# Sparse attention by query tiles: one tile and eight heads a unit, in 32-row strips

## Chip, core and metric

The kernel runs on one core of a Trainium2 chip. Its time is the device time of one launch in microseconds. A core has TensorE (matrix products into PSUM), VectorE, ScalarE, GpSimd and SyncE (which issues the transfers); each takes its own queue in order and waits on semaphores. TensorE's weight loads have rows of their own (PEld).

## What is computed

A decoder of two layers over 8 sequences of 256 tokens of 128 features. The part in question is the sparse self-attention of the second layer, 16 heads of 8 features each, on the normalised X:

```python
cols = np.arange(k_len)
rows = np.arange(k_len)[:, None]
strided = cols % STRIDE >= STRIDE - C          # STRIDE 128, C 8
local = cols[None, :] // STRIDE == rows // STRIDE
causal = cols[None, :] <= rows
layout = (strided[None, :] | local) & causal
...
qkv = hidden_states @ W_attn + b_attn
scores = jnp.where(mask, jnp.einsum('bhqd,bhkd->bhqk', q, k) * scale, mask_value)
attn = jax.nn.softmax(scores, axis=-1)
out = jnp.einsum('bhqk,bhkd->bhqd', attn, v)
return out @ W_proj + b_proj
```

A query of a sequence's first 128 tokens sees the keys before it in its own tile. A query of the second 128 sees those of its tile and, besides, the last 8 keys of the first tile: the far keys. The result is added to X and normalised.

## The kernel before

Two sequences are a group; four groups run one after the other, each with 512 tokens in four tiles of 128. A group has the stages memory attention, first mixture, sparse attention, cross-attention, second mixture. Every engine's program is written out by hand, with semaphores between them; a count waited for is the number of increments so far.

Sparse attention before (from L766 for TensorE, L1236 for ScalarE, L1834 for VectorE, L1517 for GpSimd): queries, keys and values of all tokens are made by three products of 512 columns; ScalarE writes qT (L1240) and kT (L1243), feature by token. Then a loop of eight steps runs over pairs of heads hh and hh + 8 (u is 0 and 1). For a head, VectorE masks the queries to the head's eight features (L1836), TensorE puts the mask into two banks (bf16, 272 columns, L787) and adds the scores of four tiles, 136 keys each, of which 8 are far keys (L791). VectorE takes the maxima of four tiles in one operation (L1841). ScalarE makes four exponentials of 136 columns, each with its maximum as bias and its sum as a by-product (L1249, two instructions each). TensorE turns the four tiles of probabilities (L799), ScalarE copies them out of PSUM (L1085), and TensorE multiplies them by values masked to two heads (L811), which GpSimd prepares in each step (L1519). VectorE besides keeps the reciprocals of the sums (L1847, L1851) and the far columns (L1848). After the loop the far columns (L842) and the reciprocals (L846) are turned, the far product is added, the output is scaled (L1899) and projected (L496), and moments (L1585, L1588), root (GpSimd, L1441 and L1443) and normalisation (L1593) give the next X. Behind that TensorE projects keys and values for cross-attention (L750, L756).

A fp32 product is two matmul instructions, a bf16 product or an fp32 transpose one. Cross-attention works already with 64-row pieces: scores at L872, transposes at L890.

## Time and profile before

| | |
|---|---|
| median of 3 runs | 1216.9 us (1215.03 to 1217.23) |
| profiled execution | 1212.65 us, span 1210.9 us |
| mean granted TensorE clock | 0.975 |
| busy: TensorE, VectorE, ScalarE, GpSimd | 1083.6, 736.4, 707.4, 184.4 us |
| TensorE's share of the span | 89% |
| chain that ended last | TensorE 50%, issue 32%, ScalarE 6%, VectorE 5% |

The span runs from the first to the last instruction; the time of an execution is a little longer. Busy times are sums of instructions and say nothing of the order: for that, the timeline (instructions in order of time, equal ones merged) and windows (busy time in a stretch, with the granted clock of TensorE, 1.00 at full speed) are read. A matmul's duration contains its way through the array: of a run of them, only the last one's counts in full, the others follow at a shorter distance.

### The profile page before, as it was taken

What the parts mean: (1) busy time and instruction counts of PE and PEld (TensorE: products, weight loads), DVE (VectorE), ACT (ScalarE), POOL (GpSimd) and SP (SyncE); (2) the same over time, 40 slices, a digit from 0 to 9 for tenths busy, and PEclk for the clock granted to TensorE, in tenths of its full rate; (3) what the DMA queues carried; (4) which work ended last, traced back from release to release, by engine and by line L of the source; (5) the groups of instructions that cost most, each with busy time, mean ns of one, the idle gap of its engine ahead of it and who ended that gap; (6) DMA issues with size and microseconds to landing.
All of it is one profiled execution on the core that took longest, in us unless ns stands there. A gap on an engine that the chain in (4) does not pass through costs nothing.

```text
span 1210.9 us, 23834 instructions
## 1 busy us (share of the span) xinstructions
PE 1083.6 (89%) x8477; PEld 714.9 (59%) x8477; DVE 736.4 (61%) x2015; ACT 707.4 (58%) x1913; POOL 184.4 (15%) x299
## 2 busy tenths in 40 slices
PE   3789998998989998999798999899979999899957
PEld 1564684554765487455586458555567647745546
DVE  5642575888643265788754237588874417667861
ACT  3361496775654176778455238677755507777724
POOL 4320120212120022022111012020212002200000
PEclk9899999999899999999899999999989999999979
DMA  7400000000000000000000000000000000000000
GB/s 221 138 1 1 1 0 1 11 19 2 1 11 1 0 1 1 10 19 1 2 1 10 1 1 0 1 11 19 2 1 10 1 1 1 0 1 2 2 1 9
DMA packets 21061, 15.59 MB, mean 13 GB/s; under 512 B 871, under 2 KB 18644, under 8 KB 20956
## 3 DMA queue, kind: packets, MB, share of 16 engines
q1 hardware_dynamic: 20956, 14.24, 4.0%
q8 instruction: 59, 0.97, 0.3%
q14 instruction: 46, 0.38, 0.1%
HBM read 13.18 MB, written 1.05 MB: 12 GB/s over the span
## 4 chain that ended last, share of the span: by engine, by line
PE 50%; issue 32%; ACT 6%; DVE 5%; POOL 3%; POOLq 2%; DVEq 1%; SPq 1%; DMA 0%; ACTq 0%
PE ps L718 10%; PE ps L872 5%; PE ps L791 4%; PE ps L908 4%; PE ps L756 3%; PE ps L890 3%; PE ps L750 3%; PE ps L811 2%; PE ps L799 2%; PE ps L747 2%; POOL rstd L1443 2%; ACT arena L1280 2%; PE ps L917 1%; PE ps L731 1%; DVE nmax L1911 1%
## 5 line engine op out<-in xcount | busy, mean ns | idle before, releaser
L1085 ACT ACTIVATE arena<-ps 128x512 f32<-128x512 f32 (+2 forms) x336 | 170.3, 535 | 112.7 <-PE ps L890 56.4
L1911 DVE TENSOR_REDUCE nmax<-ps 128x1 f32<-128x512 f32 x256 | 163.9, 683 | 25.0 <-PE ps L872 24.5
L1280 ACT ACTIVATE arena<-ps,nmax 128x512 f32<-128x512 f32 x256 | 173.6, 685 | 7.9 <-DVE nmax L1911 4.8
L890 PEld LDWEIGHTS ps<-ident,arena 64*128 64x128 f32 x2048 | 76.5, 138 | 82.8 <-issue 42.2
L1916 DVE COPY arena<-ps 128x512 f32<-128x512 f32 x128 | 88.2, 689 | 61.0 <-PE ps L890 61.0
L718 PE MATMUL ps<-big,w1a 128*128 128x512 f32 x256 | 117.3, 603 | 0.0
L890 PE MATMUL ps<-ident,arena 64*128 64x64 f32 x2048 | 92.4, 228 | 11.9 <-ACT arena L1085 6.3
L1249 ACT ACTIVATE arena<-ps,snm 128x136 f32<-128x136 f32 x256 | 91.8, 375 | 5.6 <-DVE snm L1841 5.6
L1441 POOL TENSOR_TENSOR vare<-mv,eps_ln 128x2 f32<-128x2 f32 x64 | 13.5, 210 | 477.0 <-DVE mv L1588 476.4
L718 PEld LDWEIGHTS ps<-big,w1a 128*128 128x128 f32 x256 | 46.3, 189 | 57.5 <-issue 56.5
L1226 ACT ACTIVATE big<-ps 128x512 f32<-128x512 f32 x16 | 9.6, 597 | 116.1 <-PE ps L718 116.1
L791 PE MATMUL ps<-kT,arena 128*128 128x136 f32 x512 | 77.2, 279 | 0.0
L1808 DVE TENSOR_TENSOR big<-XT,ps 128x512 f32<-128x512 f32 x32 | 22.0, 687 | 90.4 <-PE ps L702 90.3
L1920 DVE SCALAR_TENSOR_TENSOR X<-ps,cross_inv,X 128x128 f32<-128x128 f32 x256 | 72.5, 342 | 3.3 <-issue 0.5
L791 PEld LDWEIGHTS ps<-kT,arena 128*128 128x128 f32 x512 | 68.8, 190 | 1.8
L756 PEld LDWEIGHTS ps<-xwT,ctxT 128*128 128x128 f32 x512 | 61.9, 192 | 9.6 <-issue 9.6
L750 PE MATMUL ps<-ctxT,xwT 128*128 128x512 f32 x128 | 65.5, 626 | 0.2 <-ACT ctxT L1085 0.2
L756 PE MATMUL ps<-xwT,ctxT 128*128 128x128 f32 x512 | 64.2, 276 | 0.0
L1519 POOL TENSOR_TENSOR arena<-V,pair_mask 128x512 f32<-128x512 f32 x32 | 34.4, 1076 | 132.1 <-PE ps L811 95.9
L1841 DVE TENSOR_REDUCE snm<-ps 128x4 f32<-128x544 f32 x64 | 46.4, 724 | 11.3 <-PE ps L791 8.4
L1249 ACT ACTIVATION_READ_ACCUMULATOR arena<-ps,snm 128x1 f32 x256 | 53.1, 207 | 0.0
L1443 POOL TENSOR_TENSOR rstd<-vare,neg_half 128x2 f32<-128x2 f32 x72 | 51.1, 710 | 10.2 <-issue 0.2
(354 smaller groups left out, 2113.0 us busy)
## 6 DMA issues: line engine op xcount, KB each, us to landing
ctx<-in_ctx_dram SPq DMA_DIRECT2D x4, 512.0 KB, 4.2
w1a<-in_L_ffn_W_dram SPq DMA_DIRECT2D x1, 2048.0 KB, 9.7
w1b<-in_L_ffn_W_dram SPq DMA_DIRECT2D x1, 2048.0 KB, 12.1
w2b<-in_L_ffn_W_dram SPq DMA_DIRECT2D x8, 256.0 KB, 6.8
X<-in_x_dram SPq DMA_DIRECT2D x4, 256.0 KB, 2.8
out_dram<-Y SPq DMA_DIRECT2D x4, 256.0 KB, 2.4
arena<-in_L_xattn_Wq_dram SPq DMA_DIRECT2D x1, 512.0 KB
arena<-in_L_xattn_Wk_dram SPq DMA_DIRECT2D x1, 512.0 KB
```

The source lines that it names most:

```text
L718: last = pe.matmul(bank(acc[h]), w1a[:, e, h * P:(h + 1) * P], XE[:, e % 2, :], start=(e == 0), stop=(e == E - 1))
L750: pe.matmul(bank(b), xwT[:, 1, j, :], ctxT[:, seq * CTX:(seq + 1) * CTX], start=True, stop=True)\
L756: last = pe.matmul(ps[:, b, k * P:(k + 1) * P], ctxT[:, c * P:(c + 1) * P], xwT[:, 2, j, :], start=True, stop=True)
L791: last = pe.matmul(ps[:, o, c:c + KW], qm[:, u, b * SEQ + tq * P:b * SEQ + (tq + 1) * P], kT[:, k0:k0 + KW], start=False, stop=(tq == QT - 1))
L890: last = pe.transpose(ps[:, 4 + u, o:o + DK], cprob[r, 2 * (t % 2) + h, k * P:(k + 1) * P], ident[r, r])
L1085: return act.activation(dst, src, ACT.Copy)
L1249: last = act.activation(SP_[:, u, t, :], ps[:, 2 * u + t // QT, c:c + KW], ACT.Exp, bias=snm[:, u, t:t + 1], accum_out=srs[:, u, t:t + 1])
L1280: act.activation(cprob[:, 2 * (t % 2) + h, :], bank(2 * (t % 2) + h), ACT.Exp, bias=nmax[:, s:s + 1], accum_out=rsum[:, j % 2, s:s + 1]).t ...
L1443: return pool.tensor_tensor(result[:, r], with_eps[:, r], neg_half[:, r], ALU.pow)
L1911: dve.tensor_reduce(nmax[:, s:s + 1], bank(s % 4), AX.X, ALU.max, negate=True)\
L1916: dve.tensor_copy(cprobT[:, 2 * (t % 2), :], bank(4)).then_inc(cT_even, 1)
L1920: last = dve.scalar_tensor_tensor(out=X1[:, t, :], in0=ps[:, b, t * D:(t + 1) * D], scalar=cross_inv[:, j % 2, 2 * t + h:2 * t + h + 1], i ...
```

## The change

The loop over pairs of heads goes. The unit of work becomes one tile of 128 queries and eight heads, 1024 score columns in two banks; eight units make a group, in the tile order 1, 0, 3, 2 (SP_ORDER). The 128 features are four strips of 32 rows with four heads each (QUAD). Per tile, the keys are laid out four times, each masked to one head of every strip (km, GpSimd, the first tile by VectorE). Scores of a strip are a product over 32 rows with 512 columns, on top of the causal mask put in by a bf16 product. VectorE takes the maxima of 8 x 128 columns and subtracts them for all 1024 columns into SBUF; ScalarE makes one exponential of 1024 columns without bias and sum, in place. Far scores of all heads are one product per sequence; their maxima are joined by a minimum of negated maxima. Probabilities are turned in 64-row halves, 16 transposes a unit, into two banks, and copied by one ScalarE operation of 1024 columns. Values are masked into four tensors (VQ, GpSimd). Output columns come strip by strip in products with 32 stationary columns, once with the values and once with ones (quad_ones, head_ones), so that TensorE also makes the sums. VectorE divides tile by tile; the projection runs for a sequence when its two tiles are done. The addition of the bias to X moves from VectorE to GpSimd. The masks' setup changes accordingly. The diff, cut to the new stage:

```diff
-KW = CB + P
+STRIPS, QUAD = 4, 4
+SW = P // STRIPS
+UNITS = 2 * TT
+SP_ORDER = (1, 0, 3, 2)
...
+        SP_ = [sparse_c(2 * QUAD, P) for _ in range(2)]
+        spT = [sparse_c(2 * TOK) for _ in range(3)]
+        km = [sparse_c(QUAD * P) for _ in range(2)]
+        def by_half(view):
+            return view.rearrange("p (w h q) -> p w h q", w=2, h=2 * QUAD)
+        s_nmax = sb("s_nmax", [P, TT, NH])
+        far_nmax = sb("far_nmax", [P, GROUP, NH])
...
+                def far_scores_of():
+                    pe.wait_ge(far_keys_ready, it + 1)
                     for b in range(GROUP):
...
+                        t = b * QT + 1
+                        last = pe.matmul(ps[:, 4, b * P:(b + 1) * P], qT[:, t * P:(t + 1) * P], far_keys[:, b, :],
+                                         start=True, stop=True)
+                    last.then_inc(far_ps, 1)
+                def mask_scores(u):
+                    if u >= 2:
+                        pe.wait_ge(s_arg, it * UNITS + u - 1)
+                    for s in (2 * (u % 2), 2 * (u % 2) + 1):
+                        pe.matmul(bank(s), ident_bf[:, :], causal[:, :].unsqueeze(1).to_broadcast([P, QUAD, P]),
+                                  start=True, stop=False)
+                def scores(u):
+                    n = u // 2
+                    t = SP_ORDER[n]
+                    if n == 0:
+                        pe.wait_ge(km_first, it + 1)
+                    else:
+                        pe.wait_ge(km_ready, it * (TT - 1) + n)
+                    for s in (2 * (u % 2), 2 * (u % 2) + 1):
+                        r = slice(s * SW, (s + 1) * SW)
+                        last = pe.matmul(bank(s), qT[r, t * P:(t + 1) * P],
+                                         km[n % 2][r, :], start=False, stop=True)
                     last.then_inc(s_ps, 1)
...
+                def turn_probs(u):
+                    pe.wait_ge(s_exp, it * UNITS + u + 1)
+                    if u:
+                        pe.wait_ge(sT_ready, it * UNITS + u)
+                    else:
+                        pe.wait_ge(far_ready, it + 1)
+                    for i in range(2 * QUAD):
+                        for w in range(2):
+                            r = slice(w * DK, (w + 1) * DK)
+                            last = pe.transpose(ps[:, 4 + w, i * DK:(i + 1) * DK], SP_[u % 2][r, i, :], ident[r, r])
                     last.then_inc(sT_ps, 1)
...
+                def turn_far(n):
+                    b = SP_ORDER[n] // QT
+                    pe.wait_ge(g_exp, it * GROUP + b + 1)
+                    if n == 0:
+                        pe.wait_ge(v_ready, it + 1)
+                    else:
+                        pe.wait_ge(oT_ready, it * TT + n - 1)
+                    pe.transpose(ps[:, 6, 2 * P:3 * P], G[:, b, :], ident[:, :]).then_inc(gT_ps, 1)
+                def values(n):
+                    t = SP_ORDER[n]
+                    b, far, o = t // QT, t % QT == 1, 6 + n % 2
+                    pe.wait_ge(sT_ready, it * UNITS + 2 * n + 2)
+                    if n == 0:
+                        pe.wait_ge(vq_ready, it + 1)
+                    if n >= 2:
+                        pe.wait_ge(oT_ready, it * TT + n - 1)
+                    if far:
+                        pe.wait_ge(gT_ready, it * GROUP + b + 1)
+                    for c in (0, P):
+                        for i in range(QUAD):
+                            for s in range(STRIPS):
+                                r = slice(s * SW, (s + 1) * SW)
+                                moving = by_half(spT[(2 * n + s // 2) % 3])[:, :, (s % 2) * QUAD + i, :]
+                                last = pe.matmul(ps[r, o, c:c + P], quad_ones[:, i, :] if c else VQ[i][:, t, r], moving,
+                                                 start=(i == 0), stop=(i == QUAD - 1 and not far))
+                        if far:
+                            last = pe.matmul(ps[:, o, c:c + P],
+                                             head_ones[:, :, :].rearrange("p h c -> p (h c)") if c else Vg[:, b, :],
+                                             GT[:, b, :], start=False, stop=True)
                     last.then_inc(so_ps, 1)
...
+                def project(seq):
+                    pe.wait_ge(oT_ready, it * TT + (seq + 1) * QT)
+                    if seq == 0:
+                        pe.wait_ge(s_arg, it * UNITS + UNITS - 1)
+                    token_major_seq(1 + seq, qT, wproj[:, :], seq).then_inc(proj_ps, 1)
                 pe.wait_ge(qk_ready, it * 2 + 2)
...
+                mask_scores(0)
+                far_scores_of()
+                scores(0)
+                mask_scores(1)
+                scores(1)
+                for u in range(UNITS):
+                    n = u // 2 - 1
+                    turn_probs(u)
+                    if u % 2 == 0 and n >= 0 and SP_ORDER[n] % QT == 1:
+                        turn_far(n)
+                    if u + 2 < UNITS:
+                        mask_scores(u + 2)
+                        scores(u + 2)
+                    if u % 2 == 0 and n >= 0:
+                        values(n)
+                project(0)
+                values(TT - 1)
+                project(1)
...
+                def exps(u):
+                    act.wait_ge(s_arg, it * UNITS + u + 1)
+                    act.activation(SP_[u % 2], SP_[u % 2], ACT.Exp).then_inc(s_exp, 1)
+                def turned(u):
+                    act.wait_ge(sT_ps, it * UNITS + u + 1)
+                    if u >= 3:
+                        act.wait_ge(so_ps, it * TT + (u - 3) // 2 + 1)
+                    copy(spT[u % 3], ps[:, 4:6, :].rearrange("p b n -> p (b n)")).then_inc(sT_ready, 1)
+                def far_exps(b):
+                    act.wait_ge(g_arg, it * GROUP + b + 1)
+                    act.activation(G[:, b, :], G[:, b, :], ACT.Exp).then_inc(g_exp, 1)
+                def far_turned(b):
+                    act.wait_ge(gT_ps, it * GROUP + b + 1)
+                    copy(GT[:, b, :], ps[:, 6, 2 * P:3 * P]).then_inc(gT_ready, 1)
+                act.wait_ge(far_ps, it + 1)
+                copy(far_scores, ps[:, 4, 0:GROUP * P].rearrange("p (b n) -> p b n", b=GROUP)).then_inc(far_ready, 1)
+                exps(0)
+                for u in range(UNITS):
+                    n = u // 2
+                    if u + 1 < UNITS:
+                        exps(u + 1)
+                    if u % 2 == 0 and SP_ORDER[n] % QT == 1:
+                        far_exps(SP_ORDER[n] // QT)
+                    turned(u)
+                    if u % 2 == 0 and n and SP_ORDER[n - 1] % QT == 1:
+                        far_turned(SP_ORDER[n - 1] // QT)
...
+                def keys_of_tile(n):
+                    t = SP_ORDER[n]
+                    pool.tensor_tensor(km[n % 2].rearrange("p (i k) -> p i k", i=QUAD),
+                                       kT[:, t * P:(t + 1) * P].unsqueeze(1).to_broadcast([P, QUAD, P]),
+                                       quad_mask[:, :].unsqueeze(2).to_broadcast([P, QUAD, P]), ALU.mult)\
+                        .then_inc(km_ready, 1)
+                pool.wait_ge(qk_ready, it * 2 + 2)
+                for b in range(GROUP):
+                    k0 = b * SEQ + P - CB
+                    last = pool.tensor_tensor(far_keys[:, b, :].rearrange("p (h c) -> p h c", c=CB),
+                                              kT[:, k0:k0 + CB].unsqueeze(1).to_broadcast([P, NH, CB]),
+                                              head_mask[:, :].unsqueeze(2).to_broadcast([P, NH, CB]), ALU.mult)
+                last.then_inc(far_keys_ready, 1)
+                keys_of_tile(1)
                 pool.wait_ge(v_ready, it + 1)
...
+                by_head = "p t (h d) -> p t h d"
+                for i in range(QUAD):
+                    last = pool.tensor_tensor(VQ[i].rearrange(by_head, h=NH), V[:, :, :].rearrange(by_head, h=NH),
+                                              quad_heads[:, i:i + 1, :].unsqueeze(3).to_broadcast([P, TT, NH, HD]),
+                                              ALU.mult)
+                last.then_inc(vq_ready, 1)
+                pool.wait_ge(s_ps, it * UNITS + 2)
+                keys_of_tile(2)
+                pool.tensor_tensor(NHAT[:, :, :], X[:, :, :], bproj_bc[:, :].unsqueeze(1).to_broadcast([P, TT, D]),
+                                   ALU.add).then_inc(base_ready, 1)
+                pool.wait_ge(s_ps, it * UNITS + 4)
+                keys_of_tile(3)
...
+                def unit(u):
+                    n, w = u // 2, u % 2
+                    t = SP_ORDER[n]
+                    nm = s_nmax[:, n, w * 2 * QUAD:(w + 1) * 2 * QUAD]
+                    scored = ps[:, 2 * w:2 * w + 2, :].rearrange("p b (i k) -> p (b i) k", k=P)
+                    dve.wait_ge(s_ps, it * UNITS + u + 1)
+                    dve.tensor_reduce(nm, scored, AX.X, ALU.max, negate=True)
                     dve.drain()
...
+                    if t % QT == 1:
+                        dve.tensor_tensor(nm, nm, far_nmax[:, t // QT, w * 2 * QUAD:(w + 1) * 2 * QUAD], ALU.min)
+                        dve.drain()
+                    if u >= 2:
+                        dve.wait_ge(sT_ps, it * UNITS + u - 1)
+                    dve.tensor_tensor(SP_[u % 2], scored, nm.unsqueeze(2).to_broadcast([P, 2 * QUAD, P]), ALU.add)\
+                        .then_inc(s_arg, 1)
+                def far(n):
+                    b = SP_ORDER[n] // QT
+                    by_key = "p (h c) -> p h c"
+                    dve.tensor_tensor(G[:, b, :].rearrange(by_key, c=CB), far_scores[:, b, :].rearrange(by_key, c=CB),
+                                      s_nmax[:, n, :].unsqueeze(2).to_broadcast([P, NH, CB]), ALU.add).then_inc(g_arg, 1)
+                def divided(n):
+                    t, o = SP_ORDER[n], 6 + n % 2
+                    r = slice(t * P, (t + 1) * P)
+                    dve.wait_ge(so_ps, it * TT + n + 1)
+                    dve.reciprocal(kT[:, r], ps[:, o, P:2 * P])
+                    dve.drain()
+                    dve.tensor_tensor(qT[:, r], ps[:, o, 0:P], kT[:, r], ALU.mult).then_inc(oT_ready, 1)
+                def add_attention(seq):
+                    dve.wait_ge(proj_ps, it * GROUP + seq + 1)
+                    dve.tensor_tensor(half_of(Y, seq), half_of(NHAT, seq), half_of(tiles(1 + seq), seq), ALU.add)
+                    dve.drain()
+                    moments(Y, seq).then_inc(var_ready, 1)
+                def attended(seq):
+                    dve.wait_ge(rstd_ready, it * (LNS * GROUP) + 3 * GROUP + seq + 1)
+                    normalised(Y, X, seq).then_inc(layer_done, 1)
                 dve.wait_ge(xT_ready, it * 5 + 3)
                 for b in range(GROUP):
                     last = dve.tensor_copy(XTg[:, b, :, :], XT[:, b * SEQ + P - CB:b * SEQ + P].unsqueeze(1)
                                            .to_broadcast([P, NH, CB]))
                 last.then_inc(xg_ready, 1)
...
+                dve.wait_ge(qk_ready, it * 2 + 2)
+                t = SP_ORDER[0]
+                for i in range(QUAD):
+                    last = dve.tensor_scalar(km[0][:, i * P:(i + 1) * P], kT[:, t * P:(t + 1) * P], quad_mask[:, i:i + 1],
+                                             None, ALU.mult)
+                last.then_inc(km_first, 1)
+                dve.wait_ge(qkv_ps, it * 4 + 4)
+                dve.tensor_tensor(V[:, :, :], tiles(7), bv_bc[:, :].unsqueeze(1).to_broadcast([P, TT, D]), ALU.add)
+                dve.tensor_tensor(Vgb.rearrange("p b h d -> p b (h d)"),
                                   ps[:, 6, 0:GROUP * D].rearrange("p (b d) -> p b d", b=GROUP),
...
+                                  bv_bc[:, :].unsqueeze(1).to_broadcast([P, GROUP, D]), ALU.add).then_inc(v_ready, 1)
+                dve.wait_ge(far_ready, it + 1)
+                dve.tensor_reduce(far_nmax[:, :, :], far_scores.rearrange("p b (h c) -> p b h c", c=CB), AX.X, ALU.max,
+                                  negate=True)
+                for u in range(UNITS):
+                    unit(u)
+                    if u == 0:
+                        dve.tensor_tensor(Vg.rearrange("p b (h d) -> p b h d", h=NH), Vgb,
+                                          head_mask[:, :].unsqueeze(2).unsqueeze(1).to_broadcast([P, GROUP, NH, HD]),
+                                          ALU.mult)
+                    if u % 2 and SP_ORDER[u // 2] % QT == 1:
+                        far(u // 2)
+                    if u in (4, 6):
+                        divided((u - 4) // 2)
+                divided(2)
+                dve.wait_ge(base_ready, it + 1)
+                add_attention(0)
+                divided(3)
+                attended(0)
+                add_attention(1)
+                attended(1)
```

## Rows read from the trace of the kernel before

**Rows 1.** Windows: busy us of each engine (count), granted clock, DMA; first sparse-attention stage.

```profile
144.86:191.23 46.37, 42.75 (x394) 37.00 (x394) 32.61 (x98) 35.97 (x150) 10.48 (x12) 1.00 0.00 1
```

**Rows 2.** Timeline of that stage: start, us, engine, line, operation, count, idle before.

```profile
144.17 0.69 ACT L1243 ACTIVATE kT<-ps,cols 128x512 f32<-128x512 f32 x1 [0.17 <-PE ps L774]
...
165.52 1.09 PE L811 MATMUL ps<-arena 128*64 128x128 f32 x16
...
169.89 1.09 PE L811 MATMUL ps<-arena 128*64 128x128 f32 x16
...
186.91 0.42 DVE L1903 TENSOR_TENSOR Y<-NHAT,ps 128x256 f32<-128x256 f32 x1 [0.80 <-PE ps L496]
...
187.96 0.25 DVE L1588 BATCH_NORM_AGGREGATE mv<-bn 128x2 f32<-128x6 f32 x2
...
189.37 0.60 DVE L1593 TENSOR_SCALAR X<-Y,mv,rstd 128x128 f32<-128x128 f32 x2
...
190.63 0.60 DVE L1593 TENSOR_SCALAR X<-Y,mv,rstd 128x128 f32<-128x128 f32 x2 [0.67 <-POOL rstd L1443]
```

**Rows 3.** Groups by line and form, ScalarE: count, busy us, mean ns, idle before.

```profile
L1085 ACT ACTIVATE arena<-ps 128x512 f32<-128x512 f32 x216 | 129.1, 599 | 77.3 <-PE ps L890 56.4 <-PE ps L799 12.3 <-PE ps L756 4.5
...
L1085 ACT ACTIVATE arena<-ps 128x768 f32<-128x768 f32 x8 | 6.4, 800 | 0.0
...
L1129 ACT ACTIVATE big<-big 128x512 f32<-128x512 f32 x8 | 5.0, 631 | 0.0
```

**Rows 4.** The same groups for VectorE, and two lines of its timeline.

```profile
L1691 DVE RECIPROCAL alpha<-big 128x256 f32<-128x256 f32 x8 | 13.4, 1722 | 0.1
...
L1761 DVE TENSOR_REDUCE lg_nmax<-ps 128x1 f32<-128x768 f32 x8 | 7.7, 957 | 9.3 <-PE ps L629 9.3
...
L1761 DVE TENSOR_REDUCE lg_nmax<-ps 128x1 f32<-128x640 f32 x8 | 6.6, 824 | 17.7 <-PE ps L629 17.7
...
L1883 DVE TENSOR_TENSOR V<-ps,bv_bc 128x512 f32<-128x512 f32 x4 | 2.7, 680 | 0.0
...
359.08 0.82 DVE L1761 TENSOR_REDUCE lg_nmax<-ps 128x1 f32<-128x640 f32 x1 [2.50 <-PE ps L629]
...
359.98 0.16 DVE L1763 TENSOR_TENSOR nmax<-lg_nmax,lg_scale 128x1 f32<-128x1 f32 x1
```

**Rows 5.** TensorE's timeline: mask and scores before; cross-attention's scores and turns.

```profile
169.22 0.28 PE L787 MATMUL ps<-sparse,ident_bf 128*128 128x272 bf16 x1
...
169.33 0.63 PE L791 MATMUL ps<-kT,arena 128*128 128x136 f32 x4
...
194.41 1.99 PE L872 MATMUL ps<-X,arena 64*128 64x512 f32 x8
197.10 0.46 PE L890 MATMUL ps<-ident,arena 64*128 64x64 f32 x8 [0.70 <-ACT arena L1280]
```

**Rows 6.** GpSimd by line, and TensorE's first matmul in its timeline.

```profile
L1519 POOL TENSOR_TENSOR arena<-V,pair_mask 128x512 f32<-128x512 f32 x32 | 34.4, 1076 | 132.1 <-PE ps L811 95.9 <-DVE V L1883 36.2
...
L1510 POOL TENSOR_TENSOR nTok<-NHAT,normw_bc 128x128 f32<-128x128 f32 x16 | 6.8, 454 | 5.4 <-DVE NHAT L1754 5.4
...
13.24 0.37 PE L508 MATMUL ps<-ident,col_rows 78*128 78x78 f32 x1 [13.24 <-DMA fwr<-in_L_attn_ffn_wr_dram]
```

**Rows 7.** Windows: little of TensorE, the stretch that followed (twice); an idle one without.

```profile
298.70:300.20 1.50, 0.00 (x0) 0.00 (x0) 1.35 (x7) 0.00 (x0) 0.01 (x1) 1.00 0.00 0
300.20:310.40 10.20, 6.42 (x22) 4.69 (x23) 7.06 (x36) 4.39 (x6) 3.06 (x5) 0.50 0.00 0
643.40:645.00 1.60, 0.08 (x1) 0.00 (x0) 0.05 (x1) 0.60 (x1) 0.46 (x1) 0.99 0.58 164
645.00:648.40 3.40, 2.91 (x7) 1.78 (x8) 0.90 (x5) 1.74 (x4) 1.69 (x4) 0.50 0.01 2
354.00:356.00 2.00, 0.00 (x0) 0.00 (x0) 0.38 (x2) 0.60 (x1) 0.37 (x1) 1.00 0.45 135
```

## What the change does to the time: the prediction

> **What bounds the kernel now.** I read first the four sparse-attention stages as windows [rows 1], then one of them in order of time. In the stage shown, and to within 0.7 us in the other three, TensorE is busy 42.75 of 46.4 us, at full clock; ScalarE has 36, VectorE 32.6. So four times 46.4, 185.5 us of the 1210.9, stand to be changed, and TensorE fills 92% of them. I start a stage where kT is written (144.86 in the first) and end it where the second sequence's X is normalised (191.23), both in [rows 2]: 46.37 us. What comes before and behind stays. Inside, the loop over eight pairs of heads has a period of 4.37 us (value products start at 165.52 and 169.89 [rows 2]), 35 us in all. The reader is to see how little slack any engine has there: TensorE always finds the next head's scores to do while ScalarE makes its eight short exponentials.
>
> **What is removed.** The whole loop over pairs of heads: per group 64 short exponentials with their sums, 16 maxima, the masking of queries and values, the copies of sums and far columns. ScalarE's and VectorE's work falls. That says little about the time: the new stage has to be followed along its hand-overs, because the code allows only two units in flight and each engine takes its queue in order.
>
> **What one new unit costs.** A unit is one query tile and eight heads, 1024 columns; eight units a group.
> VectorE: the maximum of 1024 columns from PSUM. 640 took 0.824 and 768 took 0.957 us, 1.04 ns a column [rows 4], so 1.22. The subtraction: an addition from PSUM of 512 columns took 0.680 [rows 4], and with the same slope it is 1.21. With the drain between them (0.08, from an end at 359.90 to a start at 359.98 [rows 4]) a unit is 2.5 us; in the tiles that also see the far keys a minimum, like the 0.16 of a small operation [rows 4], and a drain come in, 2.75.
> ScalarE: exponential without bias, 0.631 for 512 columns; the copies took 0.599 and 0.800 for 512 and 768, 0.8 ns a column [rows 3]. So exponential 1.04, copy 1.01.
> TensorE: two bf16 mask products of 512 columns. One of 272 gives way to the next product after 0.11 us (169.22 to 169.33 [rows 5]), so 0.21 each, 0.43 for both. Scores: two fp32 calls of 512 columns, in different row strips. The 64-row calls of cross-attention run in pairs, eight matmuls (four calls) in 1.99 us of which 0.62 is the last one's length: 0.43 us per pair of matmuls, 0.87 for the unit [rows 5]. Thirty-two-row strips are not in the trace; I take them as these, with the bounds nothing and twice as much. Turning: 16 transposes; eight in cross-attention end 0.46 us after their start, 0.23 of it the last one's own length, so 0.033 apart [rows 5], so 0.53. A unit is 1.83 us.
> Value products and sums: per tile 32 fp32 calls, 64 matmuls, of 32 columns by 128. The old ones of 64 columns come 16 in 1.09 us [rows 2], 0.054 apart once one's own length of some 0.28 is taken off (four full-width fp32 score matmuls of 136 columns, 0.12 apart, end 0.63 after their start [rows 5]): two run beside each other. If four run beside each other it is 0.027; yet no weight load and matmul in the trace come closer than the 0.033 of the transposes, and I take this, 2.1 us a tile, 2.54 with the far keys' two calls. Bounds: 0.027 and 0.054 apart (1.7 and 3.5 us a tile); none beside another would be 6.9. A tile's division: reciprocal 1.722 for 256 columns, of which some 0.17 doesn't grow, as in the small operation, so 0.95 for 128 [rows 4]; with drain and product 1.32.
> GpSimd: the far keys 2 x 0.45, masked keys and values about 1.08 each [rows 6]. The four masked value tensors (4.3 us) are wanted only by the first value products, 17 us in: hidden, and the next tile's keys too. Setup operations moved on GpSimd roughly cancel: memsets and selects of the old masks go, small products for the new ones come. Its first root then shifts by under 0.5 us, and TensorE does not begin before 13.2 us, when the weights land [rows 6]: nothing.
>
> **The chain of the new stage, from kT's end.** The one rule that decides: ScalarE's queue has exponential u+1 ahead of copy u, and TensorE's transposes of u+1 wait for copy u. VectorE's next maximum waits for the scores behind these transposes. So units go round all the engines.
> (a) Far keys, their scores, first scores, hand-overs: 2.6; unit 0 2.75, the far values' mask 0.42, unit 1 2.75: 8.6 us.
> (b) Exponential 1 1.04, far exponential 0.3, copy 0 1.01, transposes, mask and scores 3 1.83 and 0.3 of hand-over, unit 3 2.5: 15.7.
> (c) Exponential 3, copy 2, far copy 0.28 (values 0 wait for it), values 0 2.54, transposes 3, mask and scores 5 1.83, unit 5 2.75, hand-overs: 25.5.
> (d) As (b), with 5 to 7: 32.6.
> (e) Exponential 7, copy 6, far copy, 35.1; values 2 37.6; division 39.2; projection 0.43 and values 3 41.8; division 43.4; projection 44.1; addition and moments 1.27, root 1.16, normalising 0.6: 47.1. The last two are from the stage before (moments' end at 188.21, normalising from 189.37 for 0.60 [rows 2]); addition and moments took 1.30 there, from 186.91 to 188.21.
> Before it is 46.4. At full clock a group is 0.7 us longer; the values' rate moves it by -1.2 to +4.0, because three value products lie on the chain. For changes of array shape, which I cannot price but by nothing and some 0.1 us each, I add 0.6: +1.3, 5 us for four groups.
> The page TensorEngine Tiling (Array Packing) of the Trainium skill, section Theoretical Speedup, puts 32-column tiles at up to four times; by it the values are 0.027 apart and the four groups come 5 us lower. No 32-column tile is in the trace.
>
> **The clock.** On this chain TensorE has about 25 us of work in 47, against 42.8 busy now. It stands idle about 2.9 us before transposes 0, 2.6 before 1, 2.6 before values 0 and 3.9 before values 2. In the kernel before, 1.5 and 1.6 us in which TensorE did almost nothing were followed by a granted clock of 0.50, its lower level (1.2 of 2.4 GHz), for 10.2 and 3.4 us [rows 7]; two more falls are like the first. Once 2 us without a matmul passed at full clock [rows 7]. With four such gaps a group I expect one or two falls in each. TensorE's share of the chain in (b) to (e) is 13.5 us, and at half clock it doubles; if 30% of it lies in such stretches it is 4 us a group, 16 in all (bounds nothing and 30).
> The page TensorE: Matmul & The Clock Gate of the Trainium skill, section on HAM oscillation, says the same of bursts between waits: the array goes back to the low clock in the pauses. The trace agrees with its 10.2 us stretches. It speaks against a change that thins out TensorE's work.
>
> **Sum.** The profiled execution took 1212.65 us, 1.75 more than its span, and lies 0.35% below the median of 1216.9; the difference of 5 + 16 = 21 is worked out on it (1234) and set on the median: 1238. As the chain's first gap may be shortened by work that I take too long, I put 1236.
>
> **Rivals.**
> Forecast, chance 0.55: bound by the hand-overs, and the clock falls: 1224 to 1250.
> The clock stays up, 0.17: 1222 (1215 to 1224). For it: the 2 us that passed unpunished. Against: four longer gaps a group.
> The narrow products do not run four beside each other, 0.13: at 0.054 apart +16 more, and the longer chain at low clock: 1250 to 1262. One at a time it would be +57 (4.7 us by three by four), which the pairs of [rows 5] speak against.
> Faster, 0.15: VectorE is the bound and not the round trip. Its work is 21 us for eight units, 5.3 for four divisions, 1 for the rest; with 2.6 ahead and 10 behind the last unit (exponential, transposes, copy, values 3, division, projection, norm), less the two divisions counted twice, a group takes 37.5 us, 9 less: 1181, and 1195 to 1208 if half of the round trips stay. It decides from where scores u+2 are ready before VectorE has done unit u+1; by my terms they come 1.7 us late once and 0.4 late later, and values 0 hold a unit back by 3 us. If the change does not give the engines the order that I read (if copy u is not behind exponential u+1), this is where it goes.
>
> **How the numbers follow.** Measuring tells no less than 0.2% from no change, 2.4 us: 1214.5 to 1219.3. Faster: 0.15, and 0.02 of the second case. Same: 0.07, the lower part of the second case. Slower: 0.76. The range leaves out most of the fourth case and the top of the third: 1206 to 1258.
>
> **What would show it.** In the windows of the changed kernel: a stage of 50 to 53 us between kT and X; TensorE busy in two thirds of it or less, idle before the first transposes of units 0 and 1 and before value products 0 and 2, waiting for ScalarE; windows with a clock of 0.50 in each stage. Exponential and copy of 1024 columns at 1.04 and 1.01, maximum at 1.22, subtraction at 1.21; 64 value matmuls in about 2.1 us. I am wrong if scores u+2 always stand before unit u+1 ends, if the clock is 1.00 throughout, or if the maxima come out clearly shorter than a slope of 1.04 ns a column.

## The result and the profile after

The changed kernel takes 1254.5 us (median of 4, 1253.0 to 1255.8) against 1216.0 beside it on the same chip: 1.032 times the time before, 95% interval [1.031, 1.034]. The direction and the range of the prediction held; the size did not: 38.5 us more, where 19 were forecast.

The profiled execution took 1254.65 us, span 1252.9, 42.0 us more than the span before. (The medians differ by only 38.5, because the profiled execution of before, 1212.65 us, lies below its median and that of after on its own.) TensorE's busy time is 1091.0 us, 7 more than before, ScalarE's 645.0 (62 less), VectorE's 740.2, the mean granted clock 0.930 instead of 0.975. The work fell where it was meant to, and the time rose.

First the four stages, from kT's end to the second X, as windows (stretch, its length, busy us of TensorE, weight loads, VectorE, ScalarE and GpSimd with counts, granted clock, DMA), then the first one cut at the ends of units 1, 3, 5 and 7, the steps (a) to (e) of the prediction:

```profile
146.64:202.03 55.39, 42.16 (x474) 24.16 (x472) 34.36 (x52) 20.18 (x26) 11.14 (x14) 0.78 0.01 1
446.33:502.22 55.89, 43.26 (x474) 24.87 (x472) 34.35 (x52) 20.17 (x25) 11.15 (x14) 0.76 0.00 1
746.60:802.55 55.95, 43.31 (x474) 24.90 (x472) 34.38 (x52) 20.18 (x25) 11.15 (x14) 0.76 0.01 1
1044.17:1099.69 55.52, 42.11 (x474) 24.26 (x472) 34.27 (x52) 20.18 (x25) 11.14 (x14) 0.78 0.01 1
...
146.64:157.57 10.93, 7.56 (x44) 2.97 (x42) 10.60 (x14) 2.73 (x4) 8.33 (x9) 0.89 0.00 0
157.57:166.57 9.00, 6.83 (x45) 3.13 (x45) 5.10 (x6) 4.13 (x5) 1.04 (x1) 0.50 0.00 0
166.57:178.36 11.79, 11.22 (x136) 6.21 (x140) 6.49 (x9) 4.21 (x5) 0.00 (x0) 0.76 0.01 3
178.36:185.58 7.22, 4.68 (x91) 2.89 (x83) 6.16 (x8) 4.13 (x5) 0.00 (x0) 1.00 0.00 0
185.58:202.03 16.45, 11.87 (x170) 8.97 (x170) 6.02 (x19) 4.97 (x7) 1.78 (x4) 0.79 0.01 2
```

These answer [rows 1]: 46.4 us at clock 1.00 have become 55.4 to 56.0 at 0.76 to 0.78. The four stages hold 37.3 of the 42.0 us (222.75 less 185.44). TensorE's 42.2 busy us are hardly fewer than the 42.75 of before, but many of them are half-clock microseconds. The granted clock is 0.50, the lower of its two levels (1.2 of 2.4 GHz), in all of (b), and in parts of (a), (c) and (e).

The second view is the timeline of the same stage, first TensorE, then VectorE: the bracket is the idle time before an entry and who ended it. It answers [rows 2, 5].

```profile
154.34 0.71 PE L827 MATMUL ps<-ident,arena 64*128 64x64 f32 x16 [2.80 <-ACT arena L1278]
...
155.75 2.07 PE L814 MATMUL ps<-arena,qT 32*128 32x512 f32 x4
160.00 1.11 PE L827 MATMUL ps<-ident,arena 64*128 64x64 f32 x16 [2.17 <-ACT arena L1116]
...
168.97 0.65 PE L854 MATMUL ps<-arena,X 128*32 128x128 f32 x8 [0.57 <-ACT q_den L1116]
...
187.98 0.66 PE L854 MATMUL ps<-arena,X 128*32 128x128 f32 x8 [3.79 <-ACT q_den L1116]
```

```profile
146.67 2.08 DVE L1939 TENSOR_SCALAR arena<-kT,quad_mask 128x128 f32<-128x128 f32 x4 [3.32 <-ACT kT L1274]
...
151.29 0.61 DVE L1900 TENSOR_TENSOR s_nmax<-s_nmax,far_nmax 128x8 f32<-128x8 f32 x1
...
153.11 1.11 DVE L1953 TENSOR_TENSOR ctx<-ctx,head_mask 128x256 f32<-128x256 f32 x1
...
155.43 0.93 DVE L1900 TENSOR_TENSOR s_nmax<-s_nmax,far_nmax 128x8 f32<-128x8 f32 x1
156.43 1.23 DVE L1904 TENSOR_TENSOR arena<-ps,s_nmax 128x1024 f32<-128x1024 f32 x1
...
164.14 1.22 DVE L1897 TENSOR_REDUCE s_nmax<-ps 128x8 f32<-128x1024 f32 x1 [3.74 <-PE ps L814]
```

TensorE's gaps stand where the prediction put them, before the turns of units 0 and 1 and before the value products of steps 0 and 2, each ended by ScalarE. The scores of unit 2 (L814) already take 2.07 us; at full clock they take 1.13. The VectorE lines hold the surprise: the masked keys, the minimum and the far values' mask take two to six times as long as beside an idle GpSimd (run 3), and [rows 4] had led to 0.16 us for the minimum.

The large operations, grouped by form (count, busy us, mean ns of one, idle before), answer [rows 3, 4]:

```profile
L1904 DVE TENSOR_TENSOR arena<-ps,s_nmax 128x1024 f32<-128x1024 f32 x32 | 39.2, 1225 | 2.4
L1897 DVE TENSOR_REDUCE s_nmax<-ps 128x8 f32<-128x1024 f32 x32 | 39.1, 1222 | 29.4 <-PE ps L814 29.3
L1917 DVE RECIPROCAL kT<-ps 128x128 f32<-128x128 f32 x16 | 15.3, 955 | 43.7 <-PE ps L857 39.8 <-PE ps L854 3.9
...
L1278 ACT ACTIVATE arena<-arena 128x1024 f32<-128x1024 f32 x32 | 33.8, 1057 | 81.7 <-DVE arena L1904 81.7
L1116 ACT ACTIVATE arena<-ps 128x1024 f32<-128x1024 f32 x32 | 32.3, 1009 | 31.9 <-PE ps L827 31.9
```

The other 4.7 us lie outside: kT of the first group ends 1.8 us later, the time from the first stage's end to the next kT is 1.7 longer, the rest is 0.7 and less. The first 1.8 are in the set-up, which the change hardly touches. TensorE there got less clock in the changed kernel (0.64, second line) than in the one before (0.80, first line). Run 10 below, whose set-up is that of the changed kernel, got 0.77 (third line) and wrote kT at 145.54 us instead of 146.64, so some 1.1 of the 1.8 us came with the execution and not with the change.

```profile
36.00:48.00 12.00, 9.54 (x56) 8.09 (x57) 5.50 (x16) 4.03 (x14) 5.38 (x9) 0.80 0.69 167
```

```profile
36.00:48.00 12.00, 10.06 (x52) 8.98 (x53) 5.22 (x16) 3.43 (x12) 5.55 (x9) 0.64 0.72 174
```

```profile
36.00:48.00 12.00, 8.83 (x53) 7.80 (x54) 6.20 (x17) 3.43 (x13) 4.82 (x8) 0.77 0.69 166
```

The 1.7 us are clock as well. Here is the way from a stage's end to the next kT, the first and the second of the kernel before, then the first of the changed one:

```profile
191.24:433.85 242.61, 224.14 (x1708) 138.63 (x1708) 148.59 (x402) 139.32 (x323) 34.19 (x54) 0.98 0.02 6
480.21:724.42 244.21, 225.99 (x1708) 139.56 (x1708) 148.72 (x402) 139.42 (x323) 34.19 (x54) 0.97 0.02 6
```

```profile
202.03:446.33 244.30, 226.29 (x1713) 140.04 (x1713) 147.97 (x401) 139.50 (x324) 34.16 (x54) 0.97 0.02 6
```

At the same place of the three, some 165 us behind the stage's end, the granted clock was 1.00 (354 to 360 us), 0.72 (643 to 649) and 0.66 (366 to 371). The kernel before had this fall on the second way alone and took 1.6 us more there. The changed kernel had it on the first as well. Run 1, with the same program there, did not, and took 242.55 us.

### The profile page after: what moved, and what is told of

It reads as the page before. It is cut to its first block, busy times and chain, and to the rows that moved or that the text cites. A ratio compares the mean times of both kernels' runs of the same rounds, so it can differ in the third digit from the quotient of the medians.

```text
span 1252.9 us, 23065 instructions
## 1 busy us (share of the span) xinstructions
PE 1091.0 (87%) x8805; PEld 671.4 (54%) x8805; DVE 740.2 (59%) x1827; ACT 645.0 (51%) x1413; POOL 186.1 (15%) x313
## 4 chain that ended last, share of the span: by engine, by line
issue 58%; PE 23%; POOL 7%; DVE 4%; ACT 4%; POOLq 2%; DVEq 1%; SPq 1%; DMA 0%; ACTq 0%
PE ps L903 4%; PE ps L939 4%; PE ps L921 3%; POOL rstd L1482 3%; PE ps L726 2%; PE ps L755 2%; ACT arena L1316 2%; DVE nmax L1971 1%; POOLq L1481 1%; PE ps L948 1%; PE ps L764 1%; PE ps L758 1%; POOL arena L1558 1%; ACT arena L1116 1%; PE ps L556 1%
## 5 line engine op out<-in xcount | busy, mean ns | idle before, releaser
L1116 ACT ACTIVATE arena<-ps 128x512 f32<-128x512 f32 (+6 forms) x300 | 162.4, 573 | 126.6 <-PE ps L921 56.5
L921 PEld LDWEIGHTS ps<-ident,arena 64*128 64x128 f32 x2048 | 76.6, 138 | 82.7 <-issue 42.3
L921 PE MATMUL ps<-ident,arena 64*128 64x64 f32 x2048 | 92.4, 228 | 11.7 <-ACT arena L1116 6.2
L1278 ACT ACTIVATE arena<-arena 128x1024 f32<-128x1024 f32 x32 | 33.8, 1057 | 81.7 <-DVE arena L1904 81.7
L1897 DVE TENSOR_REDUCE s_nmax<-ps 128x8 f32<-128x1024 f32 x32 | 39.1, 1222 | 29.4 <-PE ps L814 29.3
L1316 ACT ACTIVATION_READ_ACCUMULATOR arena<-ps,nmax 128x1 f32 x256 | 51.6, 202 | 0.0
L814 PE MATMUL ps<-arena,qT 32*128 32x512 f32 x128 | 47.5, 825 | 2.3 <-DVE arena L1939 2.3
L827 PEld LDWEIGHTS ps<-ident,arena 64*128 64x128 f32 x512 | 22.4, 163 | 47.4 <-issue 32.1
L827 PE MATMUL ps<-ident,arena 64*128 64x64 f32 x512 | 26.9, 256 | 23.5 <-ACT arena L1116 11.8
```

The source lines that it names most:

```text
L921: last = pe.transpose(ps[:, 4 + u, o:o + DK], cprob[r, 2 * (t % 2) + h, k * P:(k + 1) * P], ident[r, r])
L1116: return act.activation(dst, src, ACT.Copy)
L1316: act.activation(cprob[:, 2 * (t % 2) + h, :], bank(2 * (t % 2) + h), ACT.Exp, bias=nmax[:, s:s + 1], accum_out=rsum[:, j % 2, s:s + 1]).t ...
```

## The experiments

All stages below are measured as in the prediction, from kT's end to the second X, in each of the four groups. Each kernel was timed against the kernel before on the same chip (1214.0, 1214.5 or 1215.9 us).

**1. TensorE kept busy in the four gaps.** This asks what the clock costs. Idle products of a constant, written to a free stretch of PSUM, fill the waits and change nothing else:

```diff
+                def keep_warm(b, count):
+                    for _ in range(count):
+                        pe.matmul(ps[:, b, 3 * P:4 * P], ident_bf[:, :], causal[:, :], start=True, stop=True)
                 def turn_probs(u):
+                    if u == 0:
+                        keep_warm(5, 36)
+                    if u == 1:
+                        pe.wait_ge(v_ready, it + 1)
+                        keep_warm(7, 30)
...
+                    if n == 0:
+                        keep_warm(7, 30)
+                    if n == 2:
+                        pe.wait_ge(oT_ready, it * TT + 2)
+                        keep_warm(7, 48)
```

> The changed kernel with idle matmuls (bf16, 128 columns, into a bank that nothing else uses then) in TensorE's four long gaps of a stage: 36 before transposes 0, 30 before transposes 1, 30 before value products 0, 48 before value products 2. They wait for nothing new and their results are not used. Theory clock: the falls to 0.50 (18 and 7 us in each stage of the changed kernel) lengthen the round trip, since TensorE's 13 us on it double in part; with the clock kept up a stage falls from 55.5 us to 48.5 to 50.5, the kernel from 1254.5 to 1227 to 1235. Rival: the low clock only fills time in which TensorE would wait anyway; then the stage keeps its 55.5 us or grows by what the idle matmuls overrun, 1254 to 1260.

Measured: 1233.6 us (ratio 1.0167 [1.0150, 1.0184]). Three stages took 49.97 us at clock 1.00; the fourth 53.87 at 0.90, with some low clock left in its middle (0.74 granted from 1035 to 1055 us). The steps (a) to (e) of its first stage:

```profile
147.21:158.15 10.94, 9.69 (x98) 5.77 (x97) 10.61 (x14) 2.73 (x3) 8.34 (x9) 1.00 0.01 1
158.15:165.39 7.24, 5.53 (x61) 2.86 (x58) 5.02 (x6) 4.14 (x5) 1.04 (x1) 1.00 0.00 0
165.39:175.67 10.28, 9.77 (x164) 6.46 (x166) 6.47 (x9) 4.22 (x5) 0.00 (x0) 1.00 0.01 2
175.67:182.91 7.24, 6.08 (x120) 4.47 (x112) 6.18 (x8) 4.13 (x5) 0.00 (x0) 1.00 0.01 2
182.91:197.18 14.27, 10.99 (x193) 8.49 (x190) 5.99 (x19) 4.96 (x7) 1.78 (x4) 1.00 0.01 3
```

Against the changed kernel (b) loses 1.8 us, (c) 1.5 and (e) 2.2, together 5.4 of the stage, and (a) and (d) lose nothing. So the clock costs 5.4 to 6.0 us a stage, some 23 in all (222.75 less four times 49.97), and 3.6 us a stage over the kernel before remain at full clock.

**2. ScalarE's copy ahead of the next exponential.** The order that the prediction called the one rule that decides, undone:

```diff
                 for u in range(UNITS):
                     n = u // 2
+                    turned(u)
+                    if u % 2 == 0 and n and SP_ORDER[n - 1] % QT == 1:
+                        far_turned(SP_ORDER[n - 1] // QT)
                     if u + 1 < UNITS:
                         exps(u + 1)
                     if u % 2 == 0 and SP_ORDER[n] % QT == 1:
                         far_exps(SP_ORDER[n] // QT)
-                    turned(u)
-                    if u % 2 == 0 and n and SP_ORDER[n - 1] % QT == 1:
-                        far_turned(SP_ORDER[n - 1] // QT)
```

> ScalarE's queue in another order: copy u (and the far copy behind it) ahead of exponential u+1 instead of behind it, nothing else. Theory round trip: transposes u+1 no longer wait for exponential u+1; a stage falls by 6 us from the order alone, and by up to 10 with the gaps that feed the clock's falls gone: 1214 to 1230. Rival, VectorE or TensorE is the bound of the stage: the order moves under 1 us a stage, 1250 to 1256.

Measured: 1227.7 us (ratio 1.0111 [1.0094, 1.0128]), stages 49.3 to 49.9 at clock 0.79 to 0.83. The new order gives 6.0 to 6.2 us a stage. Not all of it need be the order itself: a mean of 0.76 to 0.78 meant 24 to 27 us at the low level in a stage, and now it is 17 to 21.

**3. GpSimd's value tiles and later keys behind VectorE's first subtractions.** This asks whether VectorE's slow operations come of GpSimd working beside them:

```diff
-                pool.wait_ge(qk_ready, it * 2 + 2)
+                pool.wait_ge(km_first, it + 1)
...
-                pool.wait_ge(v_ready, it + 1)
+                pool.wait_ge(s_arg, it * UNITS + 2)
+                keys_of_tile(2)
                 by_head = "p t (h d) -> p t h d"
...
-                pool.wait_ge(s_ps, it * UNITS + 2)
-                keys_of_tile(2)
```

> GpSimd's work taken away from beside VectorE's first operations: far keys wait until VectorE has made the first masked keys, the four masked values wait until unit 1 is subtracted. In the changed kernel the four products for the first keys take 2.08 us (0.52 each), the minima 0.61 and 0.93 and the mask of the far values 1.11, against 0.17 and 0.41 for the same forms elsewhere. Theory: they are slow because GpSimd works at the same time; the minima come to 0.17 and the mask to 0.42, a stage gains 2 to 3 us (the later far keys give back 0.5), 1242 to 1247. Rival, the forms themselves are slow: durations stay, and the kernel is 0 to 4 us slower because the masked values come later.

Measured: 1251.7 us (ratio 1.0301 [1.0282, 1.0320]), stages 55.0, 55.4, 53.2 and 54.8. VectorE's busy time a stage fell by 3 us, from 34.4 to 31.4, and every slow operation became quick: four masked keys from 2.08 to 0.87 us, minima from 0.61 and 0.93 to 0.17, the mask from 1.11 to 0.42. But the stage gained 0.4 to 0.7 us in three groups and 2.7 in one: the cause of the slow operations was shown, its worth on this kernel was missed. In the first stage the second unit's subtraction ended 1.6 us sooner, and value products 0 began 1.6 us sooner (20.7 us after kT's end instead of 22.3), yet the subtraction of unit 5 ended only 0.8 us sooner and the stage 0.4. Between them lies TensorE at half clock. One window of the changed kernel and the same of run 3:

```profile
171.00:175.00 4.00, 4.00 (x56) 2.72 (x58) 1.47 (x3) 1.98 (x2) 0.00 (x0) 0.84 0.00 0
```

```profile
171.00:175.00 4.00, 4.00 (x52) 2.29 (x41) 1.25 (x2) 1.14 (x2) 0.00 (x0) 0.76 0.00 0
```

A mean of 0.84 over 4 us means 1.3 us more at the low level, 0.76 means 1.9: the clock rose at about 172.3 and 172.9 us, 25.6 and 25.9 us after kT's end. So the work came 1.6 us sooner and the clock did not, and more of the value products ran at half speed. The other groups bear this out. In the second and fourth the clock rose within 0.3 us of where it had, and they gained 0.5 and 0.7 us; in the third it rose 3.2 us sooner behind kT's end (at 770.3 us with kT at 747.08, instead of 773.0 with kT at 746.60), and this is the group that gained 2.7. The same window of the third group, of the changed kernel and of run 3:

```profile
770.00:774.00 4.00, 4.00 (x65) 2.94 (x56) 1.42 (x2) 1.06 (x1) 0.00 (x0) 0.62 0.00 0
```

```profile
770.00:774.00 4.00, 4.00 (x58) 2.27 (x57) 1.87 (x3) 2.08 (x2) 0.00 (x0) 0.97 0.00 0
```

That this is the whole loss was not tested by itself, but run 10 bears on it too.

**4. Both.**

> Both edits of the two runs before. If round trip and the slowed start are separate parts of one chain, the gains add: 1200 to 1218, under the kernel before (1216) if the clock falls go as well. If one hides the other, it is no better than the better of the two.

Measured: 1221.8 us (ratio 1.0061 [1.0044, 1.0078]), stages 47.8 to 48.6 at clock 0.82: 0.8 to 1.9 us under run 2, in three of the four groups more than the same edit gave without the new order. The gains do add (26.8 and 2.9 us singly, 32.7 together); the range of 1200 to 1218 was missed because the late GpSimd had been put too high, as in run 3.

**5. The copy first and the gaps filled** (36, 16 and 16 idle matmuls before turns 0, 1 and value products 2).

> ScalarE's copy of a unit's transposes goes ahead of the next exponential, and idle matmuls stand before the turns of units 0 and 1 and before the value products of step 2 (36, 16 and 16 of them, results unused). Theory (the order of ScalarE's queue and TensorE's clock are two separate losses that add): the reordered kernel's stage is 49.6 us at a mean granted clock of 0.81; with the clock at 1.00 it loses another 5 to 7 us, so 43 to 45 us a stage and 1203 to 1212 us in all, below the kernel before. Rival (the two are one loss seen from two sides, since the waits that the order makes are the gaps in which the clock falls): the stage stays at 47 to 49 us even at full clock, 1219 to 1226 us in all.

Measured: 1205.6 us (ratio 0.9924 [0.9908, 0.9941]), every stage 43.86 us at clock 1.00. Order and clock are two losses: at full clock, where nothing of the clock is left to mix in, the order is worth 6.1 us a stage (49.97 to 43.86).

**6. All three** (36, 10 and 16 idle matmuls).

> The same two changes, and GpSimd's value tiles and later keys moved behind VectorE's first subtractions (36, 10 and 16 idle matmuls, fitted to the shorter gaps). Theory (with the clock up VectorE's operations beside GpSimd are on the path, so their 3 us count more than the 0.4 to 1.4 us that they gave at half clock): 2 to 3 us a stage under the kernel with the two changes alone, so about 41 to 42 us a stage and 1193 to 1201 us. Rival (the start of the stage is hidden behind other waits): 0 to 1 us a stage under it.

Measured: 1201.1 us (ratio 0.9892 [0.9875, 0.9908]).

```profile
147.01:189.48 42.47, 37.37 (x536) 23.32 (x534) 31.36 (x52) 20.60 (x25) 10.96 (x14) 1.00 0.01 2
```

1.4 us a stage under run 5, less than the 2 to 3 expected, more than the rival's 1.

**7. One gap filled, that before the turns of unit 0.**

> The changed kernel as it is, with 36 idle matmuls before the turn of unit 0 alone; the other three gaps of the stage stay. Theory (the long stretch at half clock, 18 of the 25 us a stage, comes of the first gap, and the second of the gap before the value products of step 2): the first stretch goes and the second stays, 4 us a stage less than the changed kernel's 55.7, 1236 to 1241 us. Rival (the 2.2 us gap before the turn of unit 1 makes a fall of its own): the clock falls again some microseconds later and the stage gains 0 to 1.5 us, 1247 to 1254 us.

Measured: 1255.8 us (ratio 1.0339 [1.0317, 1.0360]), stages 55.5 to 55.9: the theory fell, and the kernel does not gain even the little that the rival allowed. Three entries of TensorE's timeline and two windows say why:

```profile
154.62 0.71 PE L837 MATMUL ps<-ident,arena 64*128 64x64 f32 x16 [0.69 <-ACT arena L1293]
...
155.79 1.13 PE L815 MATMUL ps<-arena,qT 32*128 32x512 f32 x4
160.29 1.12 PE L837 MATMUL ps<-ident,arena 64*128 64x64 f32 x16 [3.37 <-ACT arena L1131]
```

```profile
150.00:160.00 10.00, 6.23 (x66) 3.41 (x64) 9.63 (x11) 3.33 (x5) 6.58 (x6) 0.95 0.00 0
160.00:173.00 13.00, 12.14 (x107) 6.49 (x111) 5.64 (x6) 5.31 (x7) 1.04 (x1) 0.51 0.00 1
```

The first fall was indeed put off: the scores of unit 2 ran at 1.13 us instead of 2.07. With that TensorE was done sooner, nobody could use it, and the wait for ScalarE's copy grew from 2.17 to 3.37 us. The clock fell in this gap, and stayed low to the same point, about 173. What was saved had been slack; what was on the chain was still at half clock.

**8. The sums twice.** In the kernel of run 6 the 16 products (32 matmuls) with quad_ones of each tile are issued a second time over the first:

```diff
+                        if c:
+                            for i in range(QUAD):
+                                for s in range(STRIPS):
...
+                                    last = pe.matmul(ps[r, o, c:c + P], quad_ones[:, i, :], moving,
+                                                     start=(i == 0), stop=(i == QUAD - 1 and not far))
```

> The kernel with all three changes, and the sums of the probabilities (32 matmuls of 32 columns' rows a query tile, quad_ones) computed twice, the second time over the first. 32 of them took 0.8 us at full clock, so 3.3 us more of TensorE a stage. Theory (at full clock TensorE is no longer what the middle of the stage waits for; only the last two tiles' sums are on the chain): 1.6 to 2 us a stage, 6 to 9 us in all above the kernel with the three changes. Rival (TensorE bounds the whole stage): all of 3.3 us a stage, 12 to 14 us in all.

Measured: 1214.0 us (ratio 1.0001 [0.9991, 1.0011]).

```profile
146.75:192.70 45.95, 40.86 (x664) 26.80 (x662) 31.45 (x52) 20.57 (x25) 10.94 (x14) 1.00 0.01 2
```

TensorE's busy time rose by 3.49 us, the stage by 3.48: the rival was right. The products of all four tiles are on the chain, not those of the last two alone, since the next turns stand behind them in TensorE's queue. The price is clean too: 128 matmuls in 3.48 us, 0.027 us apart.

**9. Three gaps filled**, that before value products 2 left.

> The changed kernel with idle matmuls in the first three gaps of the stage (before the turns of units 0 and 1 and before the value products of step 0) and none before those of step 2. With all four gaps filled a stage took 50.0 us, with the first alone 55.7, as without any. Theory (two stretches at half clock a stage, the long one of the gaps before the turns, the short one of the 3.8 us gap before the value products of step 2): the first goes and the second stays, 52 to 53 us a stage, 1239 to 1245 us in all. Rival (the falls are tied to no one gap, and the clock goes down wherever the next idle time stands): 54 to 56 us a stage, 1248 to 1256 us.

Measured: 1243.5 us (ratio 1.0230 [1.0205, 1.0254]); 52.2 to 52.4 us in three stages, 54.9 in the first, where a low stretch stayed between 155 and 175 us (0.83).

```profile
446.73:499.10 52.37, 41.77 (x570) 27.08 (x568) 34.27 (x52) 20.18 (x25) 11.16 (x14) 0.93 0.01 2
...
455.00:480.00 25.00, 21.67 (x315) 12.88 (x309) 17.83 (x22) 12.49 (x15) 2.46 (x3) 1.00 0.01 1
480.00:499.00 19.00, 13.08 (x187) 9.85 (x187) 8.25 (x20) 4.86 (x7) 1.78 (x4) 0.82 0.01 2
```

The long fall belongs to the three earlier gaps and costs 3.5 us (55.9 to 52.4), the short one to the 3.8 us gap before value products 2 and costs 2.4 (52.4 to 50.0). As run 7 shows, the gap before the turns of unit 0 filled alone does not remove the long one.

**10. GpSimd late at full clock**, with ScalarE's order of the change.

> GpSimd's late start with all four gaps filled, and ScalarE's queue in the order of the change. Theory (GpSimd's operations cost the stage 1.4 us through VectorE's start, whatever the order of ScalarE's queue): 48.3 to 49.0 us a stage against 49.97 with the gaps filled alone, 1226 to 1231 us in all. Rival (with the exponentials ahead of the copies the start is hidden, as it was in three of the four stages at half clock): 49.7 to 50.0 us a stage, 1232 to 1236 us.

Measured: 1224.3 us (ratio 1.0077 [1.0053, 1.0101]), every stage 48.34 us: 1.6 less than run 1. The group of the minima, in run 1 and in run 10:

```profile
L1915 DVE TENSOR_TENSOR s_nmax<-s_nmax,far_nmax 128x8 f32<-128x8 f32 x16 | 7.5, 469 | 1.2
```

```profile
L1914 DVE TENSOR_TENSOR s_nmax<-s_nmax,far_nmax 128x8 f32<-128x8 f32 x16 | 2.7, 167 | 1.2
```

Step (a) went from 10.9 to 9.3 us, and here all of the gain arrives. Run 3 had it at the same place and lost two thirds of it in most stages; the difference between the two kernels is the clock.

**11. The scores of unit 0 ahead of the far products**, on run 6; VectorE takes the far maximum behind the maximum of unit 0.

```diff
                 mask_scores(0)
-                far_scores_of()
                 scores(0)
+                far_scores_of()
                 mask_scores(1)
```

> The kernel with all three changes, and TensorE's scores of unit 0 ahead of the products of the far keys, whose maximum VectorE takes behind the maximum of unit 0. In the trace of the kernel with the three changes the first scores ran at 149.45 us, 1.5 us after the masked keys were ready, since the far products waited for GpSimd's far keys. Theory (the start of the stage is a chain that everything follows): the first subtraction starts about 1 us earlier and the stage is 0.7 to 1.1 us shorter than 42.47, 1196.5 to 1199 us in all. Rival (the far maximum's way over ScalarE takes its place in front of the minimum): 0 to 0.3 us a stage, 1200 to 1202 us.

Measured: 1197.0 us (ratio 0.9859 [0.9834, 0.9884]), every stage 41.31 us. TensorE in run 6, and in run 11:

```profile
148.81 0.71 PE L795 MATMUL ps<-o_max,qT 128*128 128x128 f32 x4 [0.76 <-POOL o_max L1581]
149.45 1.13 PE L815 MATMUL ps<-arena,qT 32*128 32x512 f32 x4
```

```profile
147.12 1.13 PE L815 MATMUL ps<-arena,qT 32*128 32x512 f32 x4
148.18 0.71 PE L795 MATMUL ps<-o_max,qT 128*128 128x128 f32 x4
```

kT ends at 147.01 and 146.15 us in the two, so the first scores start 2.4 and 1.0 us behind it. The stage gained 1.16: the start of the stage is a chain that everything follows. This is the fastest version, 1.4% under the kernel before.

## Why the prediction was right, and where its sizes were wrong

The steps, predicted at full clock, measured at full clock (run 1) and as the change stands:

| step | predicted, us | run 1 | changed kernel |
|---|---|---|---|
| (a) to the end of unit 1 | 8.6 | 10.94 | 10.93 |
| (b) to unit 3 | 7.1 | 7.24 | 9.00 |
| (c) to unit 5 | 9.8 | 10.28 | 11.79 |
| (d) to unit 7 | 7.1 | 7.24 | 7.22 |
| (e) to the second X | 14.5 | 14.27 | 16.45 |
| sum | 47.1 | 49.97 | 55.39 |

**What bounds the stage** was right: the hand-overs of a unit round all engines, with ScalarE's order in the middle. Taking the order away is worth 6.1 us a stage at full clock (run 5 against run 1); run 2's 6.0 to 6.2 have some clock in them.

**Operations.** Maximum 1.22 us, subtraction 1.21, exponential 1.04, copy 1.01 and reciprocal 0.95 were predicted; 1.222, 1.225, 1.057, 1.009 and 0.955 came. Slopes read from two sizes of an operation carried to 1024 columns, and two of them to another operation as well (the subtraction and the exponential).

**Steps (b) to (e)** miss by 0.1, 0.5, 0.1 and -0.2 us, together 0.5; the 0.6 us set aside for changes of array shape covers it, whatever it is made of. One term in them was too low: TensorE's part of a unit, put at 1.83 us, takes 2.24 in run 1 (turns 0.65, masks 0.53, scores 1.06, from start to start). [rows 5] give 0.46 us a pair for the scores ((1.99 - 0.62) / 3), not the 0.43 taken. In (b) the 0.3 us of hand-over took up most of that. The terms written for (b) add to 6.98, where 7.1 stands.

**Step (a) failed, by 2.3 us a stage, 9 in all.** The prediction called GpSimd's masked keys and values hidden, because nobody waits for them. Nobody does; but while GpSimd makes them, VectorE's small operations between SBUF tiles slow down, and these stand on the chain. The first maximum comes behind VectorE's masked keys, too: in run 1 it starts 3.35 us after kT's end, not 2.6, and units 0 and 1 with the far values' mask take 7.6 us, not 5.9; the two minima and the mask alone are 1.9 us longer than beside an idle GpSimd. Run 10 brings the 7.6 down to 5.7. It does not mend the start (3.63 us), since the far keys then come later; run 11, with the scores of unit 0 first, brings that to 2.1. The Trainium skill has the rule, and the prediction did not weigh it: SBUF — State Buffer, section Who interferes with whom, says that a VectorE instruction with two SBUF inputs contends with a GpSimd instruction that reads SBUF. The trace agrees for the operations that it names: minimum 0.93 against 0.17 us, mask 1.11 against 0.42, while maxima and subtractions, with an input in PSUM, kept their 1.22 and 1.23. The sentence does not cover the masked keys, with one tile and a mask column as inputs, which went from 0.87 to 2.08 us all the same.

**The narrow products** were put at 0.033 us apart; run 8 measures 0.027, the lower bound, so the rival in which they do not run four beside each other (0.13) is out. By the Trainium skill's TensorEngine Tiling (Array Packing), section Theoretical Speedup, 32-column tiles are up to four times as quick; the runs agree: products of 64 columns are 0.054 apart [rows 2], full-width ones of 136 moving columns 0.12 [rows 5]. It is 0.4 us a tile less than predicted without far keys, and the two wide far products took back more than that where they are: value products 0 and their far part hold TensorE for 2.86 us in run 1, against 2.54 predicted.

**The clock** was right in kind and too small in size. The gaps were predicted at 2.9, 2.6, 2.6 and 3.9 us and came as 2.80, 2.17, 0.57 and 3.79; the second and third are short because TensorE, at half clock, comes later itself: in run 1, filled and unfilled part together, the four are 2.9, 3.4, 2.4 and 3.9 us. "One or two falls" became two in every stage, and 4 us became 5.4 to 6.0. The term that was mis-sized is the share: 30% of TensorE's 13.5 us on the chain at half clock. The two stretches, about 155 to 173 and 186 to 193, cover (b) whole, about half of (c) and two fifths of (e). Two of the signs failed with this: a stage of 50 to 53 us, and TensorE busy in two thirds of it or less. It is busy in 76% (42.2 of 55.4), as the half-clock microseconds count as busy; at full clock, without the idle matmuls (8.7 us), it is two thirds (33.3 of 50.0, run 1). The rival that the clock stays up (0.17) is out; had it stayed up, the kernel would have taken some 1232 us (1254.5 less the 22.9 below), not 1222.

**The sum.** Four stages: 14.4 us from the chain at full clock (49.97 less 46.36, times four), of which 5 were forecast; 22.9 from the clock, of which 16 were; and 4.7 outside the stages, of which none was. 42.0 in all, against 21. All three errors went one way, and 1254.5 lies above the 1224 to 1250 of the case that was forecast. The range held since it had been drawn to 1258 for another reason, the narrow products, which were quicker than predicted: that part was luck.

**The rival "faster"** (0.15) said that without ScalarE's order the stage falls below that of before, to 37.5 us, or half of the way. That needs the full clock too. With both, 43.86 us; with GpSimd late and the scores first, 41.31. TensorE, not VectorE, is then what it runs into: it is busy 37.2 us of 41.3 (4.0 of them idle matmuls), VectorE 31.3, and extra work on it, added to run 6, came out one for one (run 8).

Left open: why the falls outside the four stages come in one execution and not in another, and what the other 1.9 us outside them are.

## What to carry to other kernels

When a change takes work off the busiest engine, follow one unit round all engines in the order of their queues, and price the stage by that chain. Then ask of each new gap in TensorE's work what clock the work behind it will get, and count the stretch to its end, not the gap; filling one gap of several may only move the wait to the next. An engine that nobody waits for is not free if it works beside small SBUF operations of another that stand on the chain.

## What was not expected of the hardware

VectorE's four products of 128 columns with a mask column (L1939) took 2.08 us beside GpSimd and 0.87 without; a minimum of 8 columns 0.61 and 0.93 instead of 0.17; a product of 256 columns 1.11 instead of 0.42. Operations with an input in PSUM kept their mean time to 0.01 us. The time lost looks like a wait rather than a slower pace: each of the eight slow minima ends within 0.04 us of the end of the GpSimd operation that was running when it began, in all four groups. These are the two of the first stage of the changed kernel, beside minima that end at 151.90 and 156.36 us:

```profile
150.80 1.07 POOL L1574 TENSOR_TENSOR Y<-V,quad_heads 128x512 f32<-128x512 f32 x1
...
155.08 1.26 POOL L1580 TENSOR_TENSOR NHAT<-X,bproj_bc 128x512 f32<-128x512 f32 x1
```

If so, a small operation loses what is left of its neighbour's 1.1 or 1.3 us. No run varied the neighbour's length, so this is not shown by experiment.

Idle matmuls, 144 a stage with 8.7 us of TensorE's time (36 in 2.18 us, 48 in 2.84), buy 5.4 to 6.0 us of a 55 us stage, where the gaps that they fill hold nothing else. Where one was left, a single gap of 3.8 us before the value products (run 9) still cost 2.4 us.
